# First units of the first product moved one slot earlier, x split ahead of the maximum, tail reordered: a fused attention and feed-forward kernel

## The chip, the cores and the metric

The kernel runs on one core of a Trainium2 chip. The metric is the device time of one execution in microseconds; lower is better. TensorE multiplies matrices, VectorE, ScalarE and GpSimd do elementwise work and reductions, and SyncE (SP) issues most of the DMAs. The engines run side by side, each through its own instructions in program order, and wait for each other at semaphores.

## The reference, cut to what matters

For 16 batches of x (128 x 256) and a context of the same shape:

```python
def attention(q, k, v, gamma):       # B, 128, 256; 8 heads of 16 rows
    qk = einsum('bhdq,bhdl->bhql', qh, kh) / sqrt(16)
    sm = softmax(qk, axis=-1)
    return gamma * einsum('bhql,bhdl->bhdq', sm, vh)

x = x + attention(layernorm(x), ctx, ctx, gamma)
n = layernorm(x)
top = argmax(softmax(n @ Wg.T), axis=-1)          # 2 experts
out0 = gelu(n @ W0a.T + b0a) @ W0b.T + b0b
out1 = relu(n @ W1a.T + b1a) @ W1b.T + b1b
x = x + where(top == 0, out0, out1)
```

Both experts have 512 hidden channels. Everything is float32.

## The kernel before, in words

Products that need the precision of float32 are made from operands split in two: a high part, rounded to a format that TensorE takes in one pass, and a low part, the rest. A product is then three matmuls: high x high, high x low, low x high.

The work is cut into slots. A batch b has four slots, j = 0 to 3, one for each pair of heads; the global number is n = 4b + j. Every engine has its own loop over n (L330, L508, L628, L816) from -7 to 63 with the work of each slot written out by hand, and a tail behind it (L361, L537, L663, L875). The row maxima of the scores, which exp needs, are made seven slots ahead: with c, k = divmod(n + 7, 4), slot n makes the maxima of batch c, pair k.

In each slot TensorE does `scores(b, j)` (L701, into the PSUM tile st) and `maxima(c, k)` (L687, the same product into smax). ScalarE takes exp of st into P (`exp`, L572), VectorE reduces smax to nmax (`take_max`, L392). st and, from batch 4 on, smax have one buffer: scores wait until exp of the slot before is done, maxima until `take_max` of the slot before is done. When batch c is complete, TensorE transposes nmax (`transpose_max`), ScalarE makes the high part mhigh (`copy_max`, L580), VectorE the low part mlow (`max_parts`, L400), and SP copies both as rows into the stacked operands (`row_copy`, L169). `scores` of the batch wait for these rows to land.

Besides that, in the slots of batch b, other batches move on:
- j = 0: `transpose_att(b-2)` (L734), behind it VectorE's `residual` (L416), which makes x1, and `moments2` of the second layernorm; GpSimd then takes the power -1/2 (`rstd`, L265).
- j = 1: `values(b-1)` (L714, into the tile od; it waits for x1 of the batch before it); VectorE's `x_norm` (L430) and `gate`.
- j = 2: `copy_od(b-1)` on ScalarE (L587, od to ods); `transpose_x(b-2)` at the end of the slot on TensorE (L751), which also waits for mlow of batch b+1.
- j = 3: `transpose_od(b-1)` (L726), VectorE's `normalise(b-1)` (L407, reciprocal and attT), ScalarE's `high_xT(b-2)` (L591, xnTh), VectorE's `low_xT(b-2)` (L448, xnTl).

The feed-forward part works on pairs i of batches 2i and 2i+1 together, in the slots of batches 2i+4 (even) and 2i+5 (odd). `gemm1(i, u)` (L761) makes unit u = 0 to 7 (128 hidden channels, units 0 to 3 of the first expert) in six matmuls. It writes the half u // 2 % 2 of the PSUM tile ff. Unit 0 waits for xnTl of both batches, units 0 and 2 wait until the results y that lay in their half have been taken. ScalarE's `hidden(i, u)` (L602) applies Gelu or Relu; units 0 to 3 run ahead of exp in j = 1, units 4 to 7 behind `copy_od` in j = 2. `high_gelu` (VectorE) and `high_relu` (ScalarE) round the hidden values, `low_hidden` (GpSimd) makes the low part. `high_pass` (L780) and `low_pass` (L798) are the second product, in j = 3 of the even batch and through the odd one; `final` (L486) on VectorE adds bias and residual, y, and SP stores it.

Before: units 0 to 3 of `gemm1` stand in j = 0 of the even batch, 4 and 5 in j = 1, 6 and 7 in j = 2. `low_xT` stands behind `normalise` in j = 3 (L532), `max_parts` from batch 4 on behind `take_max` in j = 2 (L515), `high_xT` behind exp in j = 3 (L660). `moments` (L372) adds epsilon on VectorE. SP issues the load of w1 in batch 0 and w2 in batch 1 (L213), between the rows of the maxima and the loads of x.

While n <= 15, `spin` (L676) adds matmuls on dummy data to keep TensorE busy.

## Time and profile before

| | |
|---|---|
| median of 3 runs | 233.05 us (232.76 to 233.13) |
| the profiled execution | 232.91 us |
| its span | 231.1 us |
| TensorE busy | 217.1 us, 94% |
| VectorE busy | 174.3 us, 75% |
| ScalarE busy | 145.6 us, 63% |
| GpSimd busy | 137.8 us, 60% |
| clock granted to TensorE | 1.0 throughout, that is 2.4 GHz |

The span runs from the first to the last instruction of the profiled execution; 1.8 us of its time lie around it. "Busy" is the time that an engine spent in instructions; on TensorE (PE) the ends of matmuls are modelled, and starts are the safer reading. In a row of the timeline the bracket says how long the engine was idle before, and what ended that.

### The profile page before, as it was taken

The numbers are of one execution on the slowest core, as the hardware profiler recorded it, in microseconds if no ns is written. First come the engines' busy times: TensorE is split into PE (matmuls) and PEld (weight loads), VectorE is DVE, ScalarE is ACT, GpSimd is POOL, SyncE is SP. The second block draws the span as 40 slices with busy tenths as digits, with TensorE's granted clock in tenths as the row PEclk, the third lists the DMA queues.
The fourth block names the chain that finished last, engine by engine and source line by source line (L and its number), as shares of the span: only waits on it lengthen the run. The fifth ranks groups of instructions, "written<-read, shape, count | busy, mean of one in ns | idle before, by whom it ended". The sixth has DMA issues, their size and how long they took to land.

```text
span 231.1 us, 5325 instructions
## 1 busy us (share of the span) xinstructions
PE 217.1 (94%) x2036; PEld 165.9 (72%) x2041; DVE 174.3 (75%) x357; ACT 145.6 (63%) x220; POOL 137.8 (60%) x180
## 2 busy tenths in 40 slices
PE   7789879788999999999999999999999999899995
PEld 3334445456787978788787978797879787778995
DVE  7499977999579976997699869994888444545583
ACT  6205766856985597658784779477944986624240
POOL 6852314879889718972698358934762287382800
PEclk9999999999999999999999999999999999999999
DMA  4785499543224340625052704250302000000101
GB/s 136 244 301 185 140 372 375 176 142 139 92 85 150 113 143 16 240 67 191 4 198 74 237 1 119 94 180 33 72 1 72 0 27 3 23 26 0 47 3 45
DMA packets 19393, 26.40 MB, mean 114 GB/s; under 512 B 1992, under 2 KB 12840, under 8 KB 19112
## 3 DMA queue, kind: packets, MB, share of 16 engines
q1 hardware_dynamic: 18942, 25.66, 33.4%
q10 hardware_dynamic: 426, 0.40, 0.5%
q8 instruction: 16, 0.26, 0.4%
q14 instruction: 9, 0.07, 0.1%
HBM read 11.01 MB, written 2.10 MB: 57 GB/s over the span
## 4 chain that ended last, share of the span: by engine, by line
PE 76%; DVE 8%; ACT 5%; DMA 4%; issue 3%; SPq 3%; POOL 1%
PE ff L775 20%; PE ff L795 12%; PE od L722 11%; PE st L710 10%; PE ff L807 7%; PE smax L697 5%; DVE nmax L396 3%; PE od L730 3%; DMA qkst<-mlow 2%; PE od L737 2%; PE tr L748 2%; ACT P L576 2%; PE tr L758 2%; DMA qkst<-parts 1%; PE od L679 1%
## 5 line engine op out<-in xcount | busy, mean ns | idle before, releaser
L576 ACT ACTIVATE P<-st 128x1024 f32<-128x1024 f32 x64 | 66.1, 1033 | 47.7 <-PE st L710 47.3
L396 DVE TENSOR_REDUCE nmax<-smax 128x4 f32<-128x1024 f32 x56 | 68.5, 1224 | 21.3 <-PE smax L697 20.5
L267 POOL TENSOR_TENSOR mv<-mv,power 128x1 f32<-128x1 f32 x32 | 19.1, 596 | 47.9 <-DVE mv L378 47.8
L775 PE MATMUL ff<-xnTh,w1h 128*128 128x256 f32 x128 | 38.1, 298 | 1.0 <-DVE y L495 1.0
L775 PE MATMUL ff<-xnTl,w1h 128*128 128x256 f32 x128 | 36.0, 281 | 0.0
L775 PE MATMUL ff<-xnTh,w1l 128*128 128x256 f32 x128 | 35.9, 281 | 0.0
L285 POOL TENSOR_TENSOR hidL<-hid,hidH 128x1024 fp32r<-128x1024 f32 x13 | 31.0, 2386 | 6.0 <-DVE hidH L457 4.6
L609 ACT ACTIVATE hid<-ff,b1t 128x256 f32<-128x256 f32 x64 | 26.1, 479 | 12.2 <-PE ff L775 12.1
L710 PE MATMUL st<-qkst 64*128 64x256 f32 x256 | 32.2, 330 | 1.4 <-ACT P L576 0.5
L795 PE MATMUL ff<-w2h,hidH 128*128 128x256 f32 x124 | 32.1, 292 | 0.0
L722 PE MATMUL od<-P,vt 128*32 128x256 f32 x512 | 30.9, 382 | 0.0
L795 PE MATMUL ff<-w2l,hidH 128*128 128x256 f32 x124 | 30.9, 283 | 0.0
L710 PEld LDWEIGHTS st<-qkst 64*128 64x128 f32 x256 | 19.1, 184 | 15.4 <-issue 7.1
L775 PEld LDWEIGHTS ff<-xnTh,w1h 128*128 128x128 f32 x128 | 24.1, 188 | 4.5 <-issue 2.5
L272 POOL TENSOR_TENSOR parts<-qk,parts 128x512 fp32r<-128x512 f32 x15 | 19.2, 1278 | 12.1 <-ACT parts L570 12.0
L306 POOL TENSOR_TENSOR x<-x,chosen 128x256 f32<-128x256 f32 x32 | 24.6, 768 | 2.5
L697 PE MATMUL smax<-qkst 63*128 63x256 f32 x224 | 23.1, 284 | 2.8 <-DVE nmax L396 1.5
L775 PEld LDWEIGHTS ff<-xnTl,w1h 128*128 128x128 f32 x128 | 24.1, 188 | 0.0
L775 PEld LDWEIGHTS ff<-xnTh,w1l 128*128 128x128 f32 x128 | 24.1, 188 | 0.0
L795 PEld LDWEIGHTS ff<-w2l,hidH 128*128 128x128 f32 x124 | 23.6, 190 | 0.0
L722 PEld LDWEIGHTS od<-P,vt 128*32 128x32 f32 x512 | 15.0, 109 | 11.6 <-issue 3.1
L795 PEld LDWEIGHTS ff<-w2h,hidH 128*128 128x128 f32 x124 | 23.3, 188 | 0.0
(81 smaller groups left out, 369.6 us busy)
## 6 DMA issues: line engine op xcount, KB each, us to landing
qkst<-parts SPq DMA_DIRECT2D x47, 256.0 KB
xv<-in_xv SPq DMA_DIRECT2D x16, 256.0 KB, 3.0
qk<-in_qk SPq DMA_DIRECT2D x15, 256.0 KB, 3.1
out<-y SPq DMA_DIRECT2D x16, 128.0 KB, 2.7
w1t<-in_w SPq DMA_DIRECT2D x1, 1024.0 KB, 7.2
w2t<-in_w SPq DMA_DIRECT2D x1, 1024.0 KB, 7.9
qkst<-parts ACTq DMA_DIRECT2D x1, 256.0 KB
qkst<-mlow SPq DMA_DIRECT2D x16, 8.0 KB
```

Source lines behind the costliest of these rows:

```text
L267: pool.tensor_tensor(mv[:, b % 2, 11:12], mv[:, b % 2, 10:11], power[:, 0:1], ALU.pow).then_inc(s_rstd, 1)
L272: pool.tensor_tensor(parts[:, c % 2, 0:4:3, :], qk[:, place(c, QK), :, :], parts[:, c % 2, 1:3, :], ALU.subtract).then_inc(s_lo, 1)
L285: pool.tensor_tensor(hidL[:, units, :], hid[:, units, :], hidH[:, units, :], ALU.subtract).then_inc(s_hidL, 1)
L306: pool.tensor_tensor(x1[:, b % X1, :], x1[:, b % X1, :], chosen[:, e, :], ALU.add).then_inc(s_xb, 1)
L396: dve.tensor_reduce(nmax[:, c % 2, :, :, j].rearrange("p a e -> p e a"), (ff if c in WIDE and j % 2 else smax)[:, :, :, :], AX.X, ALU.max, ...
L576: act.activation(P[:, b % 2, j, :, :, :].rearrange("p e a l -> p (e a l)"), st[:, :, :, :].rearrange("p e a l -> p (e a l)"), ACT.Exp, sca ...
L609: act.activation(hid[:, u, :], ff[:, u // 2 % 2, u % 2, :], ACT.Gelu if u < HM else ACT.Relu, bias=b1t[:, u:u + 1]).then_inc(s_hid, 1)
L697: mm = pe.matmul((ff if wide and j % 2 else smax)[:, e, a, :], qkst[rows, s, j, 0, a * 128:(a + 1) * 128], qkst[rows, s, j, 1, :], start=T ...
L710: mm = pe.matmul(st[:, e, a, :], qkst[rows, s, j, 1, a * 128:(a + 1) * 128], qkst[rows, s, j, 0, :], start=True, stop=True)
L722: mm = pe.matmul(od[32 * j:32 * j + 32, e * L:(e + 1) * L], vt[:, b % 2, HEADS * a + PAIRS * e + j, :], P[:, b % 2, j, e, a, :], start=a = ...
L775: mm = pe.matmul(ff[:, u // 2 % 2, u % 2, :], w[:, a, e, m * 128:(m + 1) * 128], xs[:, i % 2, a, :], start=a == 0 and n == 0, stop=a == LC ...
L795: pe.matmul(second(b, e), hidH[:, u, t * C:(t + 1) * C], w[:, u, :], start=u == e * HM and n == 0, stop=False)
```

## The change

- TensorE: units 0 and 1 of `gemm1` run in j = 3 of the odd batch before (in batch 3 ahead of `transpose_od`, else at the end of the slot); 2 and 3 stay in j = 0, 4 to 6 stand in j = 1, 7 in j = 2. In the tail `values(15)` comes ahead of units 2 and 3.
- ScalarE: `high_xT` stands ahead of exp of j = 3; units 4 and 5 of `hidden` ahead of exp of j = 2, 6 and 7 behind `copy_od`. It issues the loads of w1 (n = 1) and w2 (n = 5), which SP no longer does.
- VectorE: `low_xT` stands ahead of `take_max` of j = 3; `max_parts` from batch 4 on stands in j = 1, behind `gate`. In the tail `x_norm(15)` stands ahead of `low_relu`.
- Epsilon is added by GpSimd in `rstd`, and no longer by VectorE in `moments`.

The diff, cut to its core:

```diff
--- before.py
+++ after.py
@@ -130,13 +130,13 @@
         s_fill = [sem(f"s_fill{n}") for n in range(4)]
-        s_stat1, s_aggr1, s_var1, s_rstd1, s_qn = map(sem, ("s_stat1", "s_aggr1", "s_var1", "s_rstd1", "s_qn"))
+        s_stat1, s_var1, s_eps1, s_rstd1, s_qn = map(sem, ("s_stat1", "s_var1", "s_eps1", "s_rstd1", "s_qn"))
         s_hi, s_lo, s_q0, s_k0hi, s_k0lo = map(sem, ("s_hi", "s_lo", "s_q0", "s_k0hi", "s_k0lo"))
...
             sem, ("s_ods", "s_odT", "s_rden", "s_attT", "s_aT", "s_x1"))
-        s_stat2, s_aggr2, s_var2, s_rstd2, s_xn = map(sem, ("s_stat2", "s_aggr2", "s_var2", "s_rstd2", "s_xn"))
+        s_stat2, s_var2, s_eps2, s_rstd2, s_xn = map(sem, ("s_stat2", "s_var2", "s_eps2", "s_rstd2", "s_xn"))
         s_lead, s_mask, s_chosen, s_xb = map(sem, ("s_lead", "s_mask", "s_chosen", "s_xb"))
@@ -210,14 +210,12 @@
-            def load_weights(step):
+            def load_small(step):
...
                     sp.dma_start(wgb[:, :, :].rearrange("p a c -> p (a c)"), wg.partition_broadcast(128)).then_inc(s_small, 16)
-                    sp.dma_start(w1t[:, :, :, :].rearrange("p a e f -> p (a e f)"), w1).then_inc(s_w1, 16)
                 if step == 1:
-                    sp.dma_start(w2t[:, :, :].rearrange("p u l -> p (u l)"), w2).then_inc(s_w2, 16)
                     sp.dma_start(bias[:, :, :].rearrange("p e l -> p (e l)"), b2.partition_broadcast(128)).then_inc(s_bias, 16)
@@ -250,7 +248,7 @@
                 if b < 2:
-                    load_weights(b)
+                    load_small(b)
                 if b + 2 < B:
@@ -262,8 +260,10 @@
         def _(pool):
-            def rstd(b, mv, count, s_var, s_rstd):
+            def rstd(b, mv, count, s_var, s_eps, s_rstd):
                 pool.wait_ge(s_var, count)
+                pool.tensor_scalar(mv[:, b % 2, 10:11], mv[:, b % 2, 9:10], EPS, None, ALU.add).then_inc(s_eps, 1)
+                pool.wait_ge(s_eps, count)
                 pool.tensor_tensor(mv[:, b % 2, 11:12], mv[:, b % 2, 10:11], power[:, 0:1], ALU.pow).then_inc(s_rstd, 1)
@@ -309,14 +309,14 @@
             pool.wait_ge(s_const, 1)
-            rstd(0, mv1, 1, s_var1, s_rstd1)
-            rstd(1, mv1, 2, s_var1, s_rstd1)
+            rstd(0, mv1, 1, s_var1, s_eps1, s_rstd1)
+            rstd(1, mv1, 2, s_var1, s_eps1, s_rstd1)
             pool.wait_ge(s_k0hi, 1)
...
             low(1)
-            rstd(2, mv1, 3, s_var1, s_rstd1)
+            rstd(2, mv1, 3, s_var1, s_eps1, s_rstd1)
             pool.memset(identf[:, :], 0.0).then_inc(s_const, 1)
@@ -330,7 +330,7 @@
                 for c in prepared(n):
-                    rstd(c, mv1, c + 1, s_var1, s_rstd1)
+                    rstd(c, mv1, c + 1, s_var1, s_eps1, s_rstd1)
                 if j == 0 and b >= 5 and b % 2:
@@ -344,7 +344,7 @@
                 if j == 0 and b >= 2:
-                    rstd(b - 2, mv2, b - 1, s_var2, s_rstd2)
+                    rstd(b - 2, mv2, b - 1, s_var2, s_eps2, s_rstd2)
                 if j == 2 and b >= 2:
@@ -358,31 +358,29 @@
                     pool.tensor_tensor(w2l[:, units, :], w2t[:, units, :], w2h[:, units, :], ALU.subtract).then_inc(s_w2l, 1)
-            rstd(B - 2, mv2, B - 1, s_var2, s_rstd2)
+            rstd(B - 2, mv2, B - 1, s_var2, s_eps2, s_rstd2)
             masks(B - 2)
...
             low_hidden(LAST - 1, 0)
-            rstd(B - 1, mv2, B, s_var2, s_rstd2)
+            rstd(B - 1, mv2, B, s_var2, s_eps2, s_rstd2)
             masks(B - 1)
...
         def _(dve):
-            def moments(b, src, mv, count, s_stat, s_aggr, s_var):
+            def moments(b, src, mv, count, s_stat, s_var):
                 m = mv[:, b % 2, :]
...
                 dve.wait_ge(s_stat, count)
-                dve.bn_aggr(m[:, 8:10], m[:, 0:6]).then_inc(s_aggr, 1)
-                dve.wait_ge(s_aggr, count)
-                dve.tensor_scalar_add(m[:, 10:11], m[:, 9:10], EPS).then_inc(s_var, 1)
+                dve.bn_aggr(m[:, 8:10], m[:, 0:6]).then_inc(s_var, 1)
...
                     dve.wait_ge(s_qk[place(c, QK)], 16 * turn(c, QK))
-                moments(c, qk[:, place(c, QK), 0, :], mv1, c + 1, s_stat1, s_aggr1, s_var1)
+                moments(c, qk[:, place(c, QK), 0, :], mv1, c + 1, s_stat1, s_var1)
@@ -425,7 +423,7 @@
                 dve.wait_ge(s_x1, b + 1)
-                moments(b, x1[:, b % X1, :], mv2, b + 1, s_stat2, s_aggr2, s_var2)
+                moments(b, x1[:, b % X1, :], mv2, b + 1, s_stat2, s_var2)
@@ -510,9 +508,11 @@
                     final(b - 5)
+                if j == 3 and b >= 2:
+                    low_xT(b - 2)
                 if c < B:
                     take_max(c, k)
-                if (k == 0 and b < 4 or k == 1 and b >= 4) and 2 <= c <= B:
+                if k == 0 and b < 4 and 2 <= c <= B:
                     max_parts(c - 1)
@@ -526,10 +526,10 @@
                     gate(b - 2)
+                if k == 0 and b >= 4 and c <= B:
+                    max_parts(c - 1)
                 if j == 3 and b >= 1:
                     normalise(b - 1)
-                    if b >= 2:
-                        low_xT(b - 2)
                 if j == 2 and b >= 4 and b % 2 == 0:
@@ -544,8 +544,8 @@
             moments2(B - 1)
+            x_norm(B - 1)
             low_relu(LAST - 1)
-            x_norm(B - 1)
             gate(B - 1)
@@ -634,12 +634,21 @@
                             hidden((b - 4) // 2, u)
+                if j == 3 and b >= 2:
+                    high_xT(b - 2)
+                if j == 2 and b >= 4 and b % 2 == 0:
+                    for u in range(4, 6):
+                        hidden((b - 4) // 2, u)
                 if b >= 0:
...
                     row_copy(act, 0, 0)
+                if n == 1:
+                    act.dma_start(w1t[:, :, :, :].rearrange("p a e f -> p (a e f)"), w1).then_inc(s_w1, 16)
+                if n == 5:
+                    act.dma_start(w2t[:, :, :].rearrange("p u l -> p (u l)"), w2).then_inc(s_w2, 16)
                 if n in (6, 7):
@@ -654,12 +663,10 @@
                     if b >= 4 and b % 2 == 0:
-                        for u in range(4, 8):
+                        for u in range(6, 8):
                             hidden((b - 4) // 2, u)
-                if j == 3 and b >= 2:
-                    high_xT(b - 2)
-                    if b >= 4 and b % 2 == 0:
-                        high_relu((b - 4) // 2)
+                if j == 3 and b >= 4 and b % 2 == 0:
+                    high_relu((b - 4) // 2)
             for u in range(4):
@@ -837,7 +844,7 @@
                     if even:
-                        for u in range(0, 4):
+                        for u in range(2, 4):
                             gemm1((b - 4) // 2, u)
@@ -847,12 +854,11 @@
                     if even:
-                        for u in range(4, 6):
+                        for u in range(4, 7):
                             gemm1((b - 4) // 2, u)
...
                     if even:
-                        for u in range(6, 8):
-                            gemm1((b - 4) // 2, u)
+                        gemm1((b - 4) // 2, 7)
                     if odd:
@@ -866,16 +872,23 @@
                         spin(od[:, :], SPIN.get(n, 0))
+                    if b >= 3 and b % 2 == 1 and b < 5:
+                        for u in range(0, 2):
+                            gemm1((b - 3) // 2, u)
                     transpose_od(b - 1)
...
                         low_pass(b - 4, 1)
+                        for u in range(0, 2):
+                            gemm1((b - 3) // 2, u)
             transpose_att(B - 2)
-            for u in range(0, 4):
+            values(B - 1)
+            for u in range(2, 4):
                 gemm1(B // 2 - 2, u)
-            values(B - 1)
             transpose_x(B - 2, B)
...
             for u in range(4, 8):
```

## Rows read from the trace of the kernel before

**Rows 1.** The page: busy us, share of the span and instructions of TensorE.
```profile
PE 217.1 (94%) x2036; PEld 165.9 (72%) x2041; DVE 174.3 (75%) x357; ACT 145.6 (63%) x220; POOL 137.8 (60%) x180
```

**Rows 2.** Waits of TensorE: us in total, times, the longest.
```profile
PE smax L697 <- DVE nmax L396: 1.5, 2, 0.9
...
PE od L679 <- ACT ods L589: 1.3, 1, 1.3
...
PE ff L775 <- DVE y L495: 1.0, 1, 1.0
```

**Rows 3.** Timeline of TensorE, an even batch: start, us, line, out<-in, count.
```profile
136.80 0.50 PE L710 MATMUL st<-qkst 64*128 64x256 f32 x4
...
137.47 0.39 PE L775 MATMUL ff<-xnTh,w1h 128*128 128x256 f32 x1
...
139.27 0.41 PE L758 MATMUL tr<-identf,xn 128*128 128x128 f32 x2
...
142.49 0.33 PE L737 MATMUL od<-identf,attT 128*128 128x128 f32 x1
```

**Rows 4.** The chain that ended last, same batch: start, us, what.
```profile
129.58 2.84 PE ff L775 x24
...
135.26 1.61 PE ff L775 x12
```

**Rows 5.** Timeline of ScalarE, the same stretch.
```profile
137.35 1.03 ACT L576 ACTIVATE P<-st 128x1024 f32<-128x1024 f32 x1 [1.46 <-PE st L710]
138.27 0.59 ACT L589 ACTIVATE ods<-od 128x512 f32<-128x512 f32 x1
138.74 1.57 ACT L609 ACTIVATE hid<-ff,b1t 128x256 f32<-128x256 f32 x4
140.17 1.06 ACT L576 ACTIVATE P<-st 128x1024 f32<-128x1024 f32 x1
...
141.59 0.42 ACT L593 ACTIVATE xnTh<-tr 128x256 fp32r<-128x256 f32 x1
```

**Rows 6.** Timeline of VectorE, batch 3, slot 0: a low part, then a maximum.
```profile
46.20 0.43 DVE L451 TENSOR_TENSOR xnTl<-tr,xnTh 128x256 fp32r<-128x256 f32 x1 [0.21 <-ACT xnTh L593]
46.54 1.22 DVE L396 TENSOR_REDUCE nmax<-smax 128x4 f32<-128x1024 f32 x1
```

**Rows 7.** Timeline of VectorE, the stretch of rows 3.
```profile
140.39 1.23 DVE L396 TENSOR_REDUCE nmax<-smax 128x4 f32<-128x1024 f32 x1 [0.35 <-PE smax L697]
141.53 0.25 DVE L410 RECIPROCAL rden<-od 128x16 f32<-128x16 f32 x1
141.81 0.42 DVE L412 TENSOR_TENSOR attT<-od,rden 128x256 f32<-128x256 f32 x1
```

**Rows 8.** Timeline of VectorE, tail: the residual of batch 14 and its epsilon.
```profile
199.96 0.48 DVE L423 SCALAR_TENSOR_TENSOR x<-od,gam,xv 128x256 f32<-128x256 f32 x1 [0.48 <-PE od L737]
...
201.16 0.15 DVE L378 TENSOR_SCALAR mv<-mv 128x1 f32<-128x1 f32 x1
```

**Rows 9.** The chain that ended last, its beginning.
```profile
4.93 0.55 POOL mv L267
```

**Rows 10.** Timeline of ScalarE, batch 1, slot 2: the copy of w1.
```profile
32.52 1.06 ACT L645 ACTIVATE w1h<-w1t 128x1024 fp32r<-128x1024 f32 x1 [0.44 <-DMA w1t<-in_w]
```

**Rows 11.** Timeline of SP's queue: the last row of batch 1's maximum.
```profile
23.83 0.55 SPq L171 DMA_DIRECT2D qkst<-mlow  x1
```

**Rows 12.** The chain that ended last: the rows of batch 2's maximum.
```profile
30.15 5.56 DMA qkst<-mlow
```

**Rows 13.** Timeline of TensorE, the tail.
```profile
199.54 0.38 PE L737 MATMUL od<-identf,attT 128*128 128x128 f32 x2
...
206.56 0.66 PE L730 MATMUL od<-identf,ods 128*128 128x128 f32 x4 [0.35 <-ACT ods L589]
...
213.67 0.44 PE L758 MATMUL tr<-identf,xn 128*128 128x128 f32 x2 [0.54 <-DVE xn L435]
```

**Rows 14.** Timeline of TensorE, batch 1, slot 0.
```profile
26.04 0.39 PE L710 MATMUL st<-qkst 64*128 64x256 f32 x2 [0.22 <-ACT P L576]
```

## The prediction

> **What bounds the kernel now.** I read the busy table first: TensorE is busy 94% of the span [rows 1], so the question is where the other 6% sits and whether it can be touched. The waits of TensorE answer it [rows 2]: they are a handful of single events of about 1 us, none of them repeated in every batch. Two are takings of the maximum (`take_max`, L396), one is the copy of `od` to `ods` (`copy_od`, L589), one is a `y` of the tail. By the timeline nearly all of them lie before 57 us or after 185 us. Between the two TensorE runs without a break, in a period of two batches that costs the same every time. There a move of matmuls from one slot to another gains nothing by itself; it can only remove a small wait or make a new one. So I read one even batch as a timeline of three engines and ask what each slot still covers after the move.
>
> **The even batch before.** The third slot (j = 2) of b = 10 begins with its scores at 136.80, its twelve matmuls of `gemm1` begin at 137.47, the transposes of x follow at 139.27, and `transpose_att` of the next batch's first slot begins at 142.49 [rows 3]. So from the scores of slot 2 to that `transpose_att` TensorE takes 142.49 - 136.80 = 5.69 us. Twelve matmuls of `gemm1` together with their edges take 1.61 us where nothing is late [rows 4], here 139.27 - 137.47 = 1.80 us: a wait of 0.19 us, for the low part of the maximum (`max_parts`), which VectorE makes behind the maximum of the same slot. Twenty-four take 2.84 us, 0.118 us each [rows 4].
>
> **The change, part by part.**
>
> Part A, the first product. Units 0 and 1 (twelve matmuls, 1.42 us) go from the even batch's slot 0 to slot 3 of the odd batch before it, one unit (six, 0.71 us) from slot 2 to slot 1. The count is the same, and groups that follow a group of the same kind have no edge of their own, so in matmul time this costs nothing. The wait of 0.19 us goes, because `max_parts` now runs a slot earlier: -0.19 us in each even batch with maxima still to come. But the stretch of 5.69 us loses 0.71 us of cover and becomes 5.69 - 0.71 - 0.19 = 4.79 us.
>
> Part B, what must happen in that stretch. In the new order `high_xT` stands behind units 6 and 7 on ScalarE, and `low_xT` stands in front of the maximum of slot 3 on VectorE, which `normalise` follows. That is one chain from the scores of slot 2 to `transpose_att`, and each link can be read from starts. On ScalarE [rows 5]: scores to exp 137.35 - 136.80 = 0.55; exp to `copy_od` 0.92; `copy_od` to the first `hidden` 0.47; four `hidden` and on to the next activation take 140.17 - 138.74 = 1.43, so 0.36 each; two stand here now (units 4 and 5 go ahead of exp, where ScalarE has been idle 1.46 us), 0.72; then `high_xT`, 0.42. On VectorE: a start gap of 0.03; `low_xT` to the start of the maximum 0.34 [rows 6]; maximum to reciprocal 1.14, reciprocal to attT 0.28, attT 0.42 [rows 7]; a release of 0.05. Sum 0.55 + 0.92 + 0.47 + 0.72 + 0.42 + 0.03 + 0.34 + 1.14 + 0.28 + 0.42 + 0.05 = 5.34 us. TensorE would be there after 4.79 us, so it waits 0.55 us; about 0.3 us of it at the maxima of the odd batch's slot 0 (which need that same maximum), the rest at `transpose_att`. Before, `low_xT` came behind `normalise`, and none of this was in the chain. Net per even batch: +0.55 - 0.19 = +0.36 us. Five batches (4, 6, 8, 10, 12) have the whole chain: +1.8 us. In b = 14 no maximum is left, only exp behind `high_xT`; ScalarE is the later one there by a little: +0.2 us, between 0 and 0.5. Queued behind the late `high_xT` are exp of slot 3 and `high_relu`; by the same starts exp ends just as the scores of the next slot want it. Behind the late maximum stand `normalise` and nothing urgent. In the odd batch the same order costs nothing: no `hidden` stands ahead of `high_xT` there, and units 0 and 1 follow, giving 1.42 us more cover. VectorE's `high_gelu` and GpSimd's `low_hidden` are ready about when their passes come; a miss of some tenths there runs beside the 0.55 us.
>
> Part C, the epsilon. Thirty-two adds leave VectorE (0.15 us each [rows 8]) and become GpSimd operations in front of the power. The nearest price is the power itself, 0.55 us [rows 9]; zero is the other bound; I take 0.25, nearer to a plain add. On VectorE it is worth something only where VectorE is late: in batches 2 and 3 of the first 57 us four sets of moments stand between the two maxima that TensorE waits for (1.5 us together [rows 2]); 4 x 0.19 = -0.8 us. At the very start the power of batch 1 is in the chain in front of the first operands [rows 9]: +0.25 us.
>
> Part D, the weight loads. `w1` leaves SP's queue for ScalarE's, at n = 1, some 3 us sooner. ScalarE's copy of `w1` waited 0.44 us for it, in front of the `copy_od` for which TensorE waited 1.3 us [rows 10, 2]: -0.45 us, if the rows of the maximum of batch 2, which took 5.56 us behind the loads [rows 12], come sooner too. They should, since 1 MB is out of the queue ahead of them; but `w2` now starts before them. An issue took SP's queue 0.55 us [rows 11]; on ScalarE it stands behind an exp that is running and in front of one that waits for its scores, so I take nothing, at most that. Bounds of the part: +0.55 and -1.3 us.
>
> Part E, the tail. Units 0 and 1 of the seventh pair now run ahead of `transpose_att(14)`. `values(15)` follows at once and must wait for the residual: that starts 199.96 - 199.54 = 0.42 us after the transpose and takes 0.48 [rows 8, 13], so about 0.75 us of idle. The wait of 1.0 us for `y` goes [rows 2]. `copy_od(15)` stands behind `hidden` 2 and 3, whose product is now behind `values`: two activations and the copy (0.36 + 0.36 + 0.59) [rows 5] less the transposes of x leave about 1.1 us in place of 0.35 [rows 13]. Together +0.75 - 1.0 + 1.1 - 0.35 = +0.5 us. `x_norm(15)` in front of `low_relu` takes away the 0.54 us of the last transposes [rows 13], and the low part is still in time: -0.5 us. Sum 0.
>
> **Sum.** Start +0.25 - 0.45 - 0.8 = -1.0; even batches +1.8; b = 14 +0.2; tail 0: +1.0 us. The profiled execution took 232.91 us (span 231.1 and 1.8 around it), 0.14 below the median of 233.05: 233.9 us by the profile, 234.05 by the median.
>
> **The rivals.** A measurement of this kernel can tell 0.2%, 0.47 us, from no change.
>
> 1. *The pinch does not bind, faster.* If TensorE's 4.79 us are enough, because one link is shorter than read (it takes 0.55 us in eleven links; the point from which it decides is a chain of 4.8 us), the five batches give -0.19 each: -1.0 - 0.95 + 0 = -1.95, 231.1 us. For it: the chain was never run in this order, and every start is from an execution in which ScalarE had slack. Against it: the links are back to back work. Chance 0.27.
>
> 2. *Half of it.* The pinch costs 0.3 us a batch, or the start gives more than 1.0: within 0.5 us of before, 233.1 us. Chance 0.16.
>
> 3. *The loads get in the way of the rows, slower still.* The scores of batch 1 start at 26.04 and wait only for exp, by 0.22 us [rows 14], so their rows, the last issued at 23.83 [rows 11], are in by then. `w1` will be on its way at just that time. The one case of rows beside a big load took 5.56 us [rows 12]: landing at 29.4, 3.3 us late at worst, of which the waits at 34 us take back about 1. That is +2.3 at worst, +1.2 in the middle: 235.2 us, at worst 236.4. The Trainium skill (DMA: Bandwidth & Descriptors, Issuing engines are not separate DMA queues) speaks against the move: loads from another engine's queue run on the same 16 DMA engines and interleave, so only issue time is saved. By that rule the load only changes its time, and this rival is the one that it makes possible; no row here shows two loaded queues at once. Chance 0.12.
>
> That the change moves nothing is excluded: TensorE issues in program order.
>
> **How the numbers follow.** The forecast, a net cost of the pinch over the gain at the start, has 0.45 and its own range is 233.2 to 235.2. Faster by over 0.2%: rival 1 and 0.02 of rival 2, 0.29. Within: the rest of rival 2 and a little of the forecast, 0.16. Slower: 0.55. The range takes in most of rival 1 and of rival 3: 231.2 to 235.8. The predicted time is 234.0 us.
>
> **What would show it.** Right: TensorE waits for the maximum at the first maxima of every odd batch from 5 on, and for attT (L412) at `transpose_att` behind it, 0.5 to 0.6 us together, in batches 5, 7, 9, 11, 13; the idle time of VectorE in front of L451 ends with `xnTh` from ScalarE in the even batches; the period of two batches grows by 0.3 to 0.4 us. The wait of 0.44 us for `w1` is gone, and batch 4 begins about 1 us sooner. In the tail `y` is no wait any more, `values(15)` waits for `x1` and `transpose_od(15)` for `ods`. Wrong: no waits in the odd batches' slot 0 (rival 1), or a wait for a row of the maximum near 26 us (rival 3).

## The result, and the profile after

The changed kernel took 233.88 us (median of 6 runs, 233.54 to 234.61), the kernel before 233.09 us beside it (6 runs, 232.76 to 234.22): a ratio of 1.0041, interval 1.0026 to 1.0056. It is slower by 0.8 us. The forecast was 234.0 us. The profiled execution took 233.54 us with a span of 231.7 us (before: 232.91 and 231.1). Times here are medians of all executions; ratios and intervals leave out the few that fell into a slower state (below: one of 236.94 and one of 239.11 us).

The page after, its first lines (engine, busy us, share of the span, instructions):

```profile
span 231.7 us, 5330 instructions
...
PE 219.0 (95%) x2041; PEld 166.1 (72%) x2041; DVE 171.0 (74%) x325; ACT 145.4 (63%) x220; POOL 144.5 (62%) x212
```

TensorE's share is still about that of [rows 1], and says nothing of the loss. The waits of TensorE after (waiting group, what ended the wait, us in total, times, longest):

```profile
PE od L737 <- ACT ods L589: 1.2, 1, 1.2
PE st L717 <- DMA qkst<-mlow: 1.0, 1, 1.0
...
PE smax L704 <- DVE nmax L394: 0.9, 2, 0.5
PE od L686 <- ACT ods L589: 0.7, 1, 0.7
PE od L729 <- DVE x L421: 0.7, 1, 0.7
```

Against [rows 2]: the `y` wait of 1.0 us is gone, the maxima wait 0.9 instead of 1.5, the copy to `ods` at 34 us 0.7 instead of 1.3. New are a row of the maximum (`mlow`, 1.0 us, at 27 us), and two waits of the tail: `ods` 1.2 (0.35 before) and the residual 0.7. None of the lines names the loss in the even batches. It is made of pieces of 0.1 to 0.3 us, which a list of waits does not carry; the starts do. An even batch after (b = 8; it answers to [rows 3]), TensorE:

```profile
113.05 0.50 PE L717 MATMUL st<-qkst 64*128 64x256 f32 x4
...
115.54 0.66 PE L737 MATMUL od<-identf,ods 128*128 128x128 f32 x4
116.12 0.36 PE L802 MATMUL ff<-w2h,hidH 128*128 128x256 f32 x1
...
117.25 0.50 PE L717 MATMUL st<-qkst 64*128 64x256 f32 x4
117.75 0.51 PE L704 MATMUL smax<-qkst 63*128 63x256 f32 x4
118.37 0.44 PE L744 MATMUL od<-identf,attT 128*128 128x128 f32 x2
```

From the scores of slot 2 to `transpose_att` it is 118.37 - 113.05 = 5.32 us; the forecast's chain was 5.34. ScalarE and VectorE in the same stretch show that chain (in brackets: the idle time ahead, and what ended it):

```profile
113.59 1.03 ACT L576 ACTIVATE P<-st 128x1024 f32<-128x1024 f32 x1 [0.31 <-PE st L717]
114.51 0.59 ACT L589 ACTIVATE ods<-od 128x512 f32<-128x512 f32 x1
114.99 0.84 ACT L609 ACTIVATE hid<-ff,b1t 128x256 f32<-128x256 f32 x2
115.70 0.40 ACT L593 ACTIVATE xnTh<-tr 128x256 fp32r<-128x256 f32 x1
```

```profile
115.29 0.69 DVE L455 CAST hidH<-hid 128x1024 fp32r<-128x1024 f32 x1
116.14 0.42 DVE L449 TENSOR_TENSOR xnTl<-tr,xnTh 128x256 fp32r<-128x256 f32 x1 [0.16 <-ACT xnTh L593]
116.48 1.22 DVE L394 TENSOR_REDUCE nmax<-smax 128x4 f32<-128x1024 f32 x1
117.61 0.25 DVE L408 RECIPROCAL rden<-od 128x16 f32<-128x16 f32 x1
117.89 0.42 DVE L410 TENSOR_TENSOR attT<-od,rden 128x256 f32<-128x256 f32 x1
```

VectorE stood idle for 0.16 us until `xnTh` came, made the low part, then the maximum, which ended at 117.70; TensorE's maxima start at 117.75, 0.50 us behind their scores instead of the usual 0.34. `attT` ended at 118.31, and `transpose_att` starts at 118.37. A third piece was not forecast: the second product starts 0.58 us behind the transposes of `od` (115.54 to 116.12) where 0.41 is usual. It needs `hidH`, which VectorE makes at 115.29 to 115.98, ahead of the low part; with TensorE's old order, below, the start is 0.41 behind again.

Where the 0.63 us of span went, from starts that both traces have:

| stretch | before | after | difference |
|---|---|---|---|
| start to the scores of slot 18, less 0.71 us of units done sooner | 63.70 | 63.72 - 0.71 | -0.69 |
| scores of slot 18 to those of slot 58, five periods of two batches | 121.61 | 123.10 | +1.49 |
| scores of slot 58 to those of slot 60 (batch 14), with the 0.71 us again | 4.57 | 4.12 + 0.71 | +0.26 |
| `transpose_att(14)` to `transpose_od(15)`, 1.42 us of units now ahead of it | 7.02 | 6.01 + 1.42 | +0.41 |
| `transpose_od(15)` to the last transposes of x | 7.11 | 6.40 | -0.71 |

The rest, -0.13 us, lies ahead of `transpose_att(14)` (-0.04) and behind the last transposes of x (-0.09). A period, from the scores of one even batch's slot 1 to those of the next even batch's, is 24.67 us instead of 24.37: +0.30.

### The profile page after: what moved, and what is told of

Its sections match the earlier page's. It is cut to its first block, busy times and chain, and to the rows that moved or that the text cites. A ratio compares the mean times of both kernels' runs of the same rounds, so it can differ in the third digit from the quotient of the medians.

```text
span 231.7 us, 5330 instructions
## 1 busy us (share of the span) xinstructions
PE 219.0 (95%) x2041; PEld 166.1 (72%) x2041; DVE 171.0 (74%) x325; ACT 145.4 (63%) x220; POOL 144.5 (62%) x212
## 4 chain that ended last, share of the span: by engine, by line
PE 69%; ACT 13%; DVE 10%; issue 3%; DMA 3%; POOL 1%; SPq 0%; ACTq 0%; POOLq 0%
PE ff L782 18%; PE od L729 12%; PE ff L802 10%; PE st L717 8%; PE ff L814 7%; ACT P L576 6%; DVE nmax L394 5%; PE smax L704 4%; PE od L744 2%; PE tr L755 2%; PE od L737 2%; ACT ods L589 2%; PE od L686 2%; DMA qkst<-mlow 1%; ACT hid L609 1%
## 5 line engine op out<-in xcount | busy, mean ns | idle before, releaser
L265 POOL TENSOR_SCALAR mv<-mv 128x1 f32<-128x1 f32 x32 | 7.3, 229 | 42.6 <-DVE mv L376 42.6
L704 PE MATMUL smax<-qkst 63*128 63x256 f32 x224 | 23.6, 289 | 2.4 <-DMA qkst<-parts 1.3
```

Source lines behind the costliest of these rows:

```text
L704: mm = pe.matmul((ff if wide and j % 2 else smax)[:, e, a, :], qkst[rows, s, j, 0, a * 128:(a + 1) * 128], qkst[rows, s, j, 1, :], start=T ...
```

## The experiments on the even batches

Every kernel here is the changed one with the edit shown, and was timed beside the kernel before: 232.97, 232.89 and 232.93 us in the three sets. The theory is the chain above. Its rival is that the matmuls were moved at no cost and the loss is in the other engines' work.

**The order of TensorE alone put back** (slots 0, 1 and 2 of the even batch; the odd batch's slot 3 and the tail too), the other engines as changed:

```
-                        for u in range(2, 4):
+                        for u in range(0, 4):
-                        for u in range(4, 7):
+                        for u in range(4, 6):
-                        gemm1((b - 4) // 2, 7)
+                        for u in range(6, 8):
+                            gemm1((b - 4) // 2, u)
...
-                    if b >= 3 and b % 2 == 1 and b < 5:
-                        for u in range(0, 2):
-                            gemm1((b - 3) // 2, u)
...
-                        for u in range(0, 2):
-                            gemm1((b - 3) // 2, u)
             transpose_att(B - 2)
-            values(B - 1)
-            for u in range(2, 4):
+            for u in range(0, 4):
                 gemm1(B // 2 - 2, u)
+            values(B - 1)
```

> The changed kernel with TensorE's order of before: units 0 to 3 in slot 0 of the even batch, 4 and 5 in slot 1, 6 and 7 in slot 2, and the old tail of TensorE. ScalarE, VectorE and GpSimd keep the new orders. Theory: slot 2 has its 0.71 us of cover back, so the chain is covered but for some 0.25 us (hidden 6 and 7 are also later, their units end 2.3 us behind the scores): period 24.3 to 24.45 us, and the tail gains 0.4 us, in all 2.0 us off: about 231.9. Rival (the new orders of ScalarE and VectorE cost the same whatever TensorE does): period 24.6 us or more, 233.5 us.

231.93 us (12 runs), ratio 0.9964, interval 0.9938 to 0.999; the period is 24.42 us. A hit: with 0.71 us more cover in slot 2 nearly all of the +0.30 is gone. It also parts the change in two: all other engines' new order is worth -1.0 us against before (231.93 and 232.97), and TensorE's own new order costs 1.8 us on top (spans of 229.9 and 231.7 us). Of the 1.2 us of span that this version gains on before, 0.71 lie at the end (`transpose_od(15)` to the last transposes of x: 6.41 us, 6.40 after) and 0.29 ahead of slot 18. Its period is still 0.2 us longer than the shortest one found below, so the chain is not quite covered here either, as its theory had it.

**The low part behind `normalise`**, in even batches:

```
-                if j == 3 and b >= 2:
+                if j == 3 and b >= 2 and (b % 2 or b < 4):
                     low_xT(b - 2)
...
                     normalise(b - 1)
+                    if b >= 4 and b % 2 == 0:
+                        low_xT(b - 2)
```

> The changed kernel, but in the even batches from 4 on the low part of x stands behind normalise again, as before; in the odd ones it stays ahead of the maximum. The period of two batches is 24.67 us in the changed kernel and 24.37 in the one before; the waits in it are 0.17 us for hidH, 0.16 for the maximum and 0.29 for attT. Theory (the pinch is the chain scores, exp, copy of od, two hidden, high part, low part, maximum, normalise): the maximum no longer waits for ScalarE, the waits for the maximum and for attT (0.45 us) go, that for hidH stays; the period falls to 24.2 us, the time by 5 x 0.45 = 2.2 us to about 231.7, below both kernels. Rival (the cost lies in the moved units or in ScalarE's order, and VectorE only shows it): the period stays within 0.1 us of 24.67, the time within 0.5 us of 233.9.

233.43 us (12 runs), ratio 1.0011, interval 0.9994 to 1.0029; the period is 24.63. A miss: 0.04 us of a period came back, where the theory expected 0.45. Only the last of the five, 24.31 us, is much shorter; it holds batch 12, which has no `q_norm` on VectorE ahead of `hidH`. TensorE and GpSimd in it (b = 8):

```profile
118.17 0.44 PE L746 MATMUL od<-identf,attT 128*128 128x128 f32 x2
...
118.75 0.51 PE L816 MATMUL ff<-w2h,hidL 128*128 128x256 f32 x2
```

```profile
116.30 2.39 POOL L285 TENSOR_TENSOR hidL<-hid,hidH 128x1024 fp32r<-128x1024 f32 x1 [1.06 <-DVE hidH L455]
```

The scores of slot 2 start at 113.30, so the chain that I had named is indeed shorter: 4.87 us to `transpose_att` instead of 5.32. But the pass right behind it needs `hidL`, which GpSimd ends at 118.69. Two chains run side by side through this stretch, and the second is as long: scores of slot 2, VectorE's `hidH`, 2.39 us of GpSimd. The forecast had it as "ready about when their passes come".

**`high_xT` right behind `copy_od`**, ahead of units 6 and 7:

```
-                if j == 3 and b >= 2:
+                if j == 3 and b >= 2 and (b % 2 or b < 4):
                     high_xT(b - 2)
...
+                        high_xT(b - 2)
                         for u in range(6, 8):
```

> The changed kernel, but in the even batches from 4 on ScalarE makes the high part of x right behind the copy of od, ahead of hidden 6 and 7. Theory: the chain loses the two hidden (0.72 us), and is then held by VectorE, which rounds hidH until 2.9 us behind the scores; low part 0.34, maximum 1.14, reciprocal 0.28, attT 0.42 make 5.1 us in place of 5.32, so 0.2 us of the 0.45 goes in each of five batches: 24.45 us for the period, 232.9 us in all. Rival (ScalarE's order does not matter, the place of the low part alone does): no change of the period, 233.9 us.

233.35 us (12 runs), ratio 1.0017, interval 1.0003 to 1.0031, period 24.62 (the last again 24.31): a miss of the same kind. `transpose_att` comes 5.07 us behind the scores of slot 2, but GpSimd's `hidL` ends only at 119.09, and the low pass starts at 119.15. From the scores of slot 2 to that pass it is 5.51 us after, 5.45 with the low part moved and 5.46 here: the second chain sets the end in both.

**`high_gelu` a slot sooner**, so that `hidH` and `hidL` come sooner, alone and then together with the low part behind `normalise`:

```
                     gate(b - 2)
+                if j == 1 and b >= 4 and b % 2 == 0:
+                    high_gelu((b - 4) // 2)
...
-                if j == 2 and b >= 4 and b % 2 == 0:
-                    high_gelu((b - 4) // 2)
```

> The changed kernel, but high_gelu stands in slot 1 of the even batch, behind gate, where VectorE has been idle, in place of slot 2. GpSimd can then begin its low part as soon as it has added the bias, about 1.1 us sooner. Theory of two chains (from the scores of slot 2, one chain over ScalarE and VectorE ends with attT 5.3 us later, and a second over VectorE's hidH and GpSimd's hidL, 2.4 us long, ends 5.45 us later at low_pass, 0.06 us ahead of where the first one lets it begin): taking the second chain away alone gives next to nothing, the period stays within 0.1 us of 24.67 and the wait for attT stays and grows by the 0.17 us that were spent at hidH; time 233.4 to 233.9 us. Rival (GpSimd's chain is the one that binds): period 24.4 us or less, time 232.5 or less.

> The changed kernel with high_gelu in slot 1 of the even batch, and the low part of x behind normalise in the even batches from 4 on: both chains are shortened at once. Theory of two chains: the waits for hidH, the maximum, attT and hidL all go, slot 2 to transpose_att takes 4.8 to 4.85 us in place of 5.32, the period is 24.15 to 24.25 us, and the time 5 x 0.45 to 0.5 us under the changed kernel: about 231.5 us. Rival (a third thing holds the odd batch's first slot, or the two changes just add up to what they give alone, at most 0.2 us a period): period 24.5 us or more, time 233.0 or more.

Alone 240.69 us (4 runs), ratio 1.0334, interval 1.032 to 1.0347; together 236.09 us (4 runs), 1.0141, interval 1.0128 to 1.0155. Both missed by far. The first and last periods of the pair are 24.19 and 24.13 us, as expected, the three between 25.67. In those, VectorE and GpSimd read (the pair, b = 8):

```profile
116.06 2.61 DVE L388 TENSOR_SCALAR qk<-qk,mv 128x256 f32<-128x256 f32 x1
118.59 1.21 DVE L394 TENSOR_REDUCE nmax<-smax 128x4 f32<-128x1024 f32 x1
```

```profile
116.13 2.39 POOL L285 TENSOR_TENSOR hidL<-hid,hidH 128x1024 fp32r<-128x1024 f32 x1
```

`q_norm` (L388), 0.4 to 0.9 us elsewhere, takes 2.61 us when it starts beside GpSimd's `hidL`, and ends 0.15 us behind it. The maximum behind it is late, and TensorE waits 1.10 us for it. The groups of L388 tell the same (times, shortest/median/longest ns, first and last start), in the version with `high_gelu` alone moved and in the changed kernel:

```profile
L388 DVE TENSOR_SCALAR qk<-qk,mv x16: 392/612/2608, 5.0 to 156.6; 128x256 f32<-128x256 f32 x16
```

```profile
L388 DVE TENSOR_SCALAR qk<-qk,mv x16: 393/424/807, 5.1 to 149.8; 128x256 f32<-128x256 f32 x16
```

The Trainium skill (SBUF — State Buffer, SBUF: two separate sides) says that VectorE and GpSimd share a pair of ports under a lock that an instruction holds to its end. It says too that the one that starts first gets it. The trace agrees with the lock (2.61 us beside an operation of 2.39; the maxima, which read PSUM, keep their 1.21 us). With the order it agrees in part: in batch 4 of both versions `q_norm` started 0.22 us ahead of `hidL` and kept 0.42 us, but in batches 6, 8 and 10 it was first by 0.07 us, by its recorded start, and was the one that waited. Those two rows of batch 4, `high_gelu` alone moved:

```profile
65.70 0.42 DVE L388 TENSOR_SCALAR qk<-qk,mv 128x256 f32<-128x256 f32 x1
65.92 2.45 POOL L285 TENSOR_TENSOR hidL<-hid,hidH 128x1024 fp32r<-128x1024 f32 x1
```

The version with `high_gelu` alone moved lost more than the pair for a second reason: behind a wait of 1.43 us for the maximum the granted clock fell to 0.77 and 0.80 in the stretches 120 to 124 and 124 to 128 us, and its third and fourth periods are 27.46 us (the second, at full clock, 26.01). The pair, with waits of 1.10 us, held 1.00 there.

Batches 4 and 12 have no clash, and so test the two chains cleanly. From the scores of slot 2 to `transpose_att` they take 5.33 us with `high_gelu` alone moved, as in the changed kernel (5.32), and 4.79 us in the pair. With the low part alone moved the pass behind `transpose_att` starts at 5.46 us in batch 4, and in batch 12, where no `q_norm` stands ahead of `hidH`, at 5.12; in the pair it starts at 4.98 in both. So in batch 4 neither repair alone gives the time back, and both together do.

**`q_norm` out of the way**: the pair, and the even batches' `q_norm` behind `high_gelu`, where GpSimd has no long operation:

```
                 for p in prepared(n - 1):
-                    q_norm(p)
+                    if b < 4 or b % 2:
+                        q_norm(p)
...
                     high_gelu((b - 4) // 2)
+                    for p in prepared(n):
+                        q_norm(p)
```

> As the kernel with both chains shortened, whose normalisation of q in slot 2 took 2.61 us beside GpSimd's low part of the hidden values (116.06 to 118.67, GpSimd 116.13 to 118.52) in place of 0.40; here that one VectorE operation stands in slot 1 of the even batch too, ahead of max_parts. Theory (the two engines shut each other out, and that alone spoilt the shortening): every normalisation of q takes under 0.9 us, no wait of TensorE stays in batches 4 to 13, the period is 24.15 to 24.25 us in place of 25.67, and the time about 231.5 us. Rival (GpSimd's earlier low part slows the maxima or another operation of VectorE as well): period 24.6 us or more.

231.63 us (12 runs), ratio 0.995, interval 0.992 to 0.9981. A hit: all periods are 24.18 to 24.20 us, 0.17 below before, and the `q_norm` that was moved takes 0.41 us (those of the odd batches 0.87):

```profile
111.17 0.41 DVE L388 TENSOR_SCALAR qk<-qk,mv 128x256 f32<-128x256 f32 x1
```

So the two chains together make the loss of the even batches. With both shortened, and TensorE's new order kept, only a gain is left, -0.17 us a period. It fits the wait for `max_parts` that no longer exists, for which rival 1 had -0.19.

## The experiments on the start

**`w1` sooner or back.** First at n = -1 instead of 1; then, in another version, both loads on SP's queue in their old places:

```
-                if n == 1:
+                if n == -1:
                     act.dma_start(w1t[:, :, :, :].rearrange("p a e f -> p (a e f)"), w1).then_inc(s_w1, 16)
```

> The changed kernel, but ScalarE issues the load of w1 at n = -1 in place of n = 1, some 2 us sooner. In the changed kernel the scores of batch 1 (n = 4) begin at 27.01, 0.97 us later than before, waiting for the rows of the maximum beside that load; by n = 8 the loss is gone. Theory A (the load delays the rows, and the loss is real): scores of batch 1 begin at about 26.2, and since the rows of batch 2 are then issued sooner too, batch 2 begins 0.5 to 0.8 us sooner and the time falls to about 233.2. Theory B (the loss is taken back anyway, since batch 2 waits for its rows beside w2 in any case): the scores of batch 1 are sooner, batch 2 is not, and the time stays within 0.3 us of 233.9.

```
+                    sp.dma_start(w1t[:, :, :, :].rearrange("p a e f -> p (a e f)"), w1).then_inc(s_w1, 16)
                 if step == 1:
+                    sp.dma_start(w2t[:, :, :].rearrange("p u l -> p (u l)"), w2).then_inc(s_w2, 16)
...
-                if n == 1:
-                    act.dma_start(w1t[:, :, :, :].rearrange("p a e f -> p (a e f)"), w1).then_inc(s_w1, 16)
-                if n == 5:
-                    act.dma_start(w2t[:, :, :].rearrange("p u l -> p (u l)"), w2).then_inc(s_w2, 16)
```

> The changed kernel with both weight loads on SP's queue at their old places. In four kernels with the loads on ScalarE's queue the rows of batch 1 landed at 27 us in place of 25.5 and its scores began at 27.0 to 27.3, and those of batch 2 began anywhere from 35.8 to 37.2. Theory (the moved loads delay the rows and gain nothing): scores of batch 1 at 26.2, batch 2 at 35.7 to 35.9, the start no later than in the changed kernel: time 233.3 to 233.9 us, less spread over the runs. Rival (the earlier w1 gives the 0.45 us that the prediction counted): batch 2 begins later than 36.2 and the time is 234.2 or more.

Back: 233.79 us (5 runs), ratio 1.0039, interval 1.0026 to 1.0052, the time of the changed kernel, as the theory expected. The scores of slot 4, after and with the loads back:

```profile
27.01 0.39 PE L717 MATMUL st<-qkst 64*128 64x256 f32 x2 [1.04 <-DMA qkst<-mlow]
```

```profile
26.08 0.39 PE L715 MATMUL st<-qkst 64*128 64x256 f32 x2 [0.21 <-ACT P L578]
```

The rows of batch 1's maximum came 1 us late while `w1` was on its way, and with the loads back they do not. But the scores of slot 8 start at 35.81 after and at 36.02 here (before: 35.75). What the moved loads cost at 27 us they give back by 36. With the loads back ScalarE waits 0.64 us for `w1`, which lands at 32.72, TensorE 1.4 us for the `ods` behind it, and 0.4 us for the rows of batch 2:

```profile
32.74 1.06 ACT L652 ACTIVATE w1h<-w1t 128x1024 fp32r<-128x1024 f32 x1 [0.64 <-DMA w1t<-in_w]
```

In the changed kernel `w1` lands at 27.90 and ScalarE does not wait for it; TensorE waits 0.7 us for `ods`, and not at all for the rows of batch 2. On balance the move is worth nothing. The Trainium skill (DMA: Bandwidth & Descriptors, Issuing engines are not separate DMA queues) has the rule that the queues of two engines share the 16 DMA engines and only issue time is saved. That agrees: the load on ScalarE's queue delayed rows on SP's by 1 us, and the time is the same to 0.1 us.

Sooner: 236.32 us (6 runs), ratio 1.0127, interval 1.0092 to 1.0161, a miss of every theory. The rows of batch 1 landed no sooner, at 27.2 us, those of batch 2 later; the scores of slot 8 start at 37.24. And TensorE slowed in the profiled execution (236.22 us). Windows of 4 us (their length; busy us of TensorE, its weight loads, VectorE, ScalarE, GpSimd; then the granted clock, the DMA share, GB/s):

```profile
34.00:38.00 4.00, 2.13 (x17) 1.41 (x15) 1.98 (x4) 3.22 (x6) 0.80 (x1) 0.94 0.94 325
38.00:42.00 4.00, 4.00 (x31) 2.18 (x31) 3.06 (x5) 2.10 (x3) 1.04 (x3) 0.63 0.63 219
```

The same windows after:

```profile
34.00:38.00 4.00, 3.14 (x22) 1.91 (x24) 3.21 (x5) 3.77 (x5) 1.06 (x1) 1.00 0.87 280
38.00:42.00 4.00, 4.00 (x53) 2.28 (x54) 3.86 (x12) 2.06 (x3) 3.08 (x7) 1.00 0.59 204
```

TensorE was busy for 2.13 us of the four, then the granted clock fell, to a mean of 0.63; 31 matmuls stand where 53 do. For part of that window the clock was at the lower of its two levels, 1.2 GHz: three dummy matmuls take 1.46 us there, and 0.82 at 2.4 GHz. The fall is not the whole loss: two executions of this version kept the full clock to 0.1% and took 234.96 and 235.58 us.

**The epsilon on VectorE again**, with the loads as changed, and with the loads back:

```
-                pool.tensor_scalar(mv[:, b % 2, 10:11], mv[:, b % 2, 9:10], EPS, None, ALU.add).then_inc(s_eps, 1)
-                pool.wait_ge(s_eps, count)
...
-                dve.bn_aggr(m[:, 8:10], m[:, 0:6]).then_inc(s_var, 1)
+                dve.bn_aggr(m[:, 8:10], m[:, 0:6]).then_inc(s_aggr, 1)
+                dve.wait_ge(s_aggr, count)
+                dve.tensor_scalar_add(m[:, 10:11], m[:, 9:10], EPS).then_inc(s_var, 1)
```

> The changed kernel with epsilon on VectorE again and only the power on GpSimd. Theory (GpSimd's extra operation costs 0.15 us at the very start, VectorE's adds cost 0.19 us each where VectorE is late in batches 2 and 3): scores of batch 0 at 19.45, batch 2 to batch 4 0.5 to 0.8 us longer, time 234.2 to 234.6 us. Rival (the waits for the maximum in batches 2 and 3 went for another reason, such as the low part of x ahead of the maximum): the start to batch 4 takes as long as in the changed kernel and the time is 233.6 to 233.9 us.

> The changed kernel with the loads on SP's queue (233.79 us when measured) and epsilon on VectorE too; the same step with the loads on ScalarE's queue gave 234.46, but with a wait of 2.2 us for the rows of batch 1 in its profile. Theory A (the epsilon that leaves VectorE is what shortened batches 2 and 3, the 0.8 us of the prediction): from the scores of n = 8 to those of n = 18 28.4 us or more in place of 27.81, time 234.4 us. Theory B (it is nearly free there, as 65.95 - 37.97 = 27.98 in the disturbed profile suggests): 27.8 to 28.0 us, and the time stays within 0.3 us of 233.79.

With the loads as changed 234.46 us (7 runs), ratio 1.0074, interval 1.0048 to 1.01. The time is what the theory expected, but not for its reason: from slot 8 to slot 18 it takes 27.98 us, 27.91 after. The time is spread from 233.7 to 235.9, and in the profiled execution (235.89 us) slot 4 waited 2.15 us for its row and the clock fell behind that. With the loads back it is 233.78 us (12 runs), ratio 1.0038, interval 1.0018 to 1.0058, against 233.79 with the epsilon on GpSimd. Its profile is of one of the two executions that took about 235 us. From slot 8 to slot 18 it has 29.04 us, which taken alone would speak for theory A; but the excess lies between slots 8 and 10, where the granted clock was 0.78 to 0.80. From the scores of slot 10 to those of slot 18, at full clock, it takes 23.02 us with the epsilon on VectorE and 23.04 after. The epsilon is worth nothing that these runs can tell.

**The first low part back behind `normalise`** in batch 2, loads back too:

```
-                if j == 3 and b >= 2:
+                if j == 3 and b >= 3:
                     low_xT(b - 2)
...
                     normalise(b - 1)
+                    if b == 2:
+                        low_xT(0)
```

> The changed kernel with the loads on SP's queue, and the low part of x of batch 0 behind normalise in slot 3 of batch 2, as before. In the kernel before TensorE waited 0.9 us for it there, in front of the dummy matmuls of batch 3. Theory (that is where the start gained, not on the epsilon): the wait of 0.9 us for xnTl is back, n = 8 to n = 18 takes 0.5 to 0.8 us longer than 27.81, time 234.3 to 234.6 us. Rival (the gain is spread over the moments of VectorE): within 0.2 us of 27.81 and of 233.79.

233.55 us (12 runs), ratio 1.0023, interval 1.0004 to 1.0042; 10 to 18 takes 23.03 us. The theory missed: there is no loss, so the place of the low part does not make the gain either.

What is left is read, not run by itself. From slot 10 to slot 18 the kernel before took 23.19 us, and would take 23.90 with the 0.71 us of units; after takes 23.04, a gain of 0.86. Of it 0.28 us lie between the scores of slots 12 and 13: 2.57 us before, 2.29 after. ScalarE before and after:

```profile
45.25 0.64 ACT L570 ACTIVATE parts<-qk 128x512 fp32r<-128x512 f32 x1
45.77 0.39 ACT L593 ACTIVATE xnTh<-tr 128x256 fp32r<-128x256 f32 x1
```

```profile
43.56 0.39 ACT L593 ACTIVATE xnTh<-tr 128x256 fp32r<-128x256 f32 x1
```

Before, `high_xT(0)` stood behind an exp, the copy of `w2` and the parts, at 45.77; VectorE's low part followed, and TensorE stood idle for it until 46.77. After, it runs at 43.56, and the scores of slot 13 wait 0.23 us for exp instead. The version with TensorE's old order has the 2.29 us too (and 22.54 us from 10 to 18, with 0.71 less of units), so it is not TensorE's order. Another 0.32 us lie between slots 10 and 12 (4.65 us before, 4.33 after), at a wait for a maximum (0.88 and 0.42 us); the version with TensorE's old order has the 4.33 us too. The last 0.27 us lie behind slot 15, and with TensorE's old order only 0.06 of them are there. The cause of both stays open.

## A version that beats both

The version with `q_norm` aside, the loads back on SP's queue, and in the tail `copy_od(15)` ahead of units 2 and 3:

```
-            for u in range(4):
+            for u in range(2):
                 hidden(LAST - 1, u)
             copy_od(B - 1)
+            for u in range(2, 4):
+                hidden(LAST - 1, u)
```

> The same, with the weight loads on SP's queue at their old places and, in the tail, the copy of od of batch 15 ahead of hidden 2 and 3. Theory: the tail loses its wait of 1.2 us for ods (transpose_att(14) to transpose_od(15) takes 4.85 us in place of 6.01), the rest is as in the kernel that it is built on, the loads change only the spread: about 230.4 us, 1.1% below the kernel before. Rival (the tail is held by another wait next, such as the low part of x or hidH): no less than 231.2 us.

230.25 us (6 runs), ratio 0.9874, interval 0.9847 to 0.9902: 1.3% below before, and a hit. Its tail on TensorE, and that of the changed kernel:

```profile
199.55 0.38 PE L749 MATMUL od<-identf,attT 128*128 128x128 f32 x2
200.60 1.93 PE L734 MATMUL od<-P,vt 128*32 128x256 f32 x32 [0.67 <-DVE x L423]
...
204.20 0.60 PE L742 MATMUL od<-identf,ods 128*128 128x128 f32 x4
```

```profile
201.98 0.38 PE L744 MATMUL od<-identf,attT 128*128 128x128 f32 x2
203.03 1.93 PE L729 MATMUL od<-P,vt 128*32 128x256 f32 x32 [0.67 <-DVE x L421]
...
207.99 0.66 PE L737 MATMUL od<-identf,ods 128*128 128x128 f32 x4 [1.20 <-ACT ods L589]
```

From `transpose_att(14)` to `transpose_od(15)` it is 4.65 us instead of 6.01: the 1.20 us of waiting for `ods` are gone; the 0.67 us for the residual stay. From there to the last transposes of x it is 6.68 us instead of 6.40, so 1.1 us are left of the gain. This edit was run only as a part of this version.

## Why the prediction was right, and where its steps were not

- **What bounds** (two TensorE runs without a break, so a move of matmuls only removes or makes a small wait): right. Putting TensorE's order back alone took 1.8 us away, with the same matmuls.
- **Part B, the chain of 5.34 us against 4.79 of cover**: right to 0.02 us (5.32), and the net +0.36 a batch came out as +0.30. The places were right too: the maximum and `attT`. Batch 14 cost +0.26 (forecast +0.2).
- **"ready about when their passes come"**, of `high_gelu` and `low_hidden`: this sentence failed. The second chain is only some tenths shorter, and with the first one shortened it binds. The time was not touched by that, but the advice that one would have taken from it was: of two repairs of the named chain, each gave back 0.05 us or less in four of five periods (0.36 in the last).
- **Part A, -0.19 us**: right, seen as -0.17 a period once nothing pinches.
- **Part C, the epsilon, -0.8 us in batches 2 and 3**: the wrong cause. The gain is there (-0.86 from slot 10 to slot 18), and the epsilon has no part in it that the runs show. The nearest that the traces give (read, not run alone) is that for 0.28 us of it VectorE was late for `xnTh`, which stood behind other work on ScalarE. I had taken every wait for VectorE as VectorE's own count of operations. The prices around it were near: on GpSimd one add takes 0.23 us (forecast 0.25), and the scores of slot 0 start 0.15 us later (forecast 0.25).
- **Part D, -0.45 us**: failed as a sum. The load's move is worth nothing (233.79 and 233.88 us). The gain that it names did come: the wait for `w1` is gone, that for `ods` shorter by 0.6 us, and the rows of batch 2 are in time. But rival 3's wait, its sign of the forecast being wrong, came too (1.0 us at 27 us; the rival had +1.2 in its middle), and the two cancel by slot 8 (35.81 us after, 36.02 with the loads back, 35.75 before). The forecast had counted the gain without the price.
- **The start as a sum**: -1.0 forecast, -0.69 measured, with the gain that was laid to the epsilon and nothing from the loads.
- **Part E, the tail**: the waits were right one by one: residual 0.67 (0.75), `ods` 1.20 (1.1), +0.41 us for both less `y` (+0.5), and -0.71 behind (-0.5); -0.3 in all where the forecast had 0. The place of `x_norm(15)`, to which the forecast laid the last of these, was not run by itself.
- **Rival 1** (no pinch, 231.1 us) is near what the kernel with both chains shortened does: 231.63.

The sum was right by its largest term, and by some luck: the start gave 0.3 us less than forecast, and the even batches cost 0.3 us less (+1.49 for +1.8). Of the terms at the start the largest had the right size and the wrong cause.

## What to carry to other kernels

Where an engine runs without a break, measure for each slot the cover that stays after a move, and sum each chain that has to fit under it, not only the one that the edit touches: a second chain of nearly the same length makes a repair of the first worth next to nothing (here 0.04 us a period). Read such losses from starts in one period, since a list of waits leaves out pieces of a tenth or two. And before an operation of VectorE is moved, see which long operation of GpSimd will then run beside it.

## What was not expected of the hardware

- `q_norm` on VectorE, SBUF to SBUF, 128 x 256: 0.4 us by itself, 2.61 us when it started 0.07 us ahead of GpSimd's 2.39 us operation, by the trace's times, and 0.42 us when it started 0.22 us ahead. The maximum behind it, from PSUM, kept 1.21 us.
- A load of 1 MB issued on another engine's queue made small rows land late enough for a wait of 1.04 us (2.15 us in one other execution), and issuing it sooner did not bring them sooner.
- The granted clock fell behind waits in some executions: after 2.13 us of work in 4, a window at a mean of 0.63, in which TensorE did 31 matmuls instead of 53; after a wait of 1.43 us in mid-kernel, windows at 0.77 and 0.80, but no fall one period earlier behind the same kind of wait; none after waits of 1.10 us. A late row can cost more than its wait: with `w1` sooner slot 8 starts 1.43 us later than in the changed kernel (37.24 and 35.81), and slot 9 2.16 us later (39.99 and 37.83).
